# A graph network with attention and a tree of experts: fewer zero columns among the edge matmuls, zero matmuls behind the edges, and epsilon inside ScalarE's root

## The reference

```
xn = layernorm(x)
x1 = x + gnn(xn, 10000 random edges) + linear_attention(xn)
out = x1 + tree(layernorm(x1))

gnn, three layers:
    hn  = h @ Wn + bn
    m   = hn[src] + edge_attr @ We + be        # one row an edge
    agg = segment_sum(m, dst) / max(count, 1)
    h   = relu(layernorm(concat(hn, agg) @ Wc + bc) * gamma + beta)     # eps = 1e-5

tree: every row goes down 8 levels of a binary tree of 255 nodes; at each node it met it is
multiplied by that node's 256x256 matrix, weighted by gelu(|score|), and summed.
```

## Time and profile before

| | |
|---|---|
| median of 3 runs | 392.23 us (392.08 to 395.37) |
| the profiled execution, its own time | 393.82 us |
| its span, first to last instruction | 392.1 us |
| mean granted TensorE clock (1 is full) | 0.987 |
| PE busy | 357.6 us (91%) |
| DVE busy | 249.1 us (64%) |
| ACT busy | 149.5 us (38%) |
| POOL busy | 120.0 us (31%) |
| the chain that ended last: PE, DVE, DMA, ACT | 83%, 8%, 3%, 1% |

### The profile page before, as it was taken

One profiled execution on the slowest core, in us unless ns is written; L12 is line 12 of the kernel. 1 busy time (PEld: TensorE's weight loads), 2 busy tenths in 40 slices (PEclk: granted clock), 3 DMA queues, 4 the chain that ended last, 5 costly groups with the idle time before them and its releaser, 6 DMA issues.

```text
span 392.1 us, 9600 instructions
## 1 busy us (share of the span) xinstructions
PE 357.6 (91%) x2773; PEld 258.4 (66%) x2773; DVE 249.1 (64%) x678; ACT 149.5 (38%) x470; POOL 120.0 (31%) x241
## 2 busy tenths in 40 slices
PE   0599999999799999999977899999999999899966
PEld 0457778998688788876633466656656665566645
DVE  1637859991524335186796776669986666568732
ACT  1325536400301405004613356544556655444510
POOL 7200000700000000062650255456545554455510
PEclk9999999999899999998999899999999999999999
DMA  6931115730499900000071269999999999997001
GB/s 198 268 103 43 40 32 125 189 95 5 160 388 387 387 22 0 0 2 0 0 264 12 103 233 386 386 386 385 385 361 381 384 386 386 385 386 281 3 3 65
DMA packets 51785, 78.48 MB, mean 200 GB/s; under 512 B 3260, under 2 KB 19223, under 8 KB 51736
## 3 DMA queue, kind: packets, MB, share of 16 engines
q1 hardware_dynamic: 50506, 76.81, 56.3%
q10 hardware_dynamic: 1230, 1.05, 1.0%
HBM read 77.21 MB, written 0.64 MB: 199 GB/s over the span
## 4 chain that ended last, share of the span: by engine, by line
PE 83%; DVE 8%; issue 3%; DMA 3%; ACT 1%; SPq 1%; DVEq 1%; POOLq 0%; POOL 0%; ACTq 0%
PE ps L1280 80%; DMA reg<-in_L_gnn_Wc_dram 3%; PE ps L1283 2%; DVE reg L1270 1%; DVE reg L908 1%; DVE reg L1274 1%; DVE cols L1140 0%; SPq L401 0%; DVE reg L1134 0%; DVE reg_w L1220 0%; DVEq L361 0%; DVE colp L1146 0%; ACT reg L615 0%; DVE reg L1220 0%; ACT reg_w L624 0%
## 5 line engine op out<-in xcount | busy, mean ns | idle before, releaser
L1280 PE MATMUL ps<-reg 128*64 128x256 f32 (+6 forms) x1449 | 253.2, 315 | 7.0 <-DVE reg L1270 3.6
L1280 PEld LDWEIGHTS ps<-reg 128*64 128x64 f32 (+5 forms) x1449 | 176.1, 146 | 24.1 <-issue 7.8
L1280 PE MATMUL ps<-reg,reg_w 128*64 (+1 forms) x688 | 158.8, 388 | 4.9 <-DVE reg L1220 2.7
L1280 PEld LDWEIGHTS ps<-reg,reg_w 128*64 128x64 f32 (+1 forms) x688 | 94.2, 140 | 59.1 <-issue 14.9
L583 POOL TENSOR_TENSOR reg_w<-reg_w 128x128 f32 x150 | 72.9, 486 | 88.8 <-ACT reg_w L804 81.5
L1220 DVE SCALAR_TENSOR_TENSOR reg_w<-reg_w,nid,reg 128x128 f32 x167 | 65.4, 395 | 33.6 <-PE ps L1280 30.6
L803 ACT COPY reg_w<-ps 64x128 f32<-64x128 f32 x150 | 39.4, 262 | 68.4 <-PE ps L1280 68.3
L1220 DVE SCALAR_TENSOR_TENSOR reg<-reg_w,reg 128x128 f32 x150 | 50.9, 339 | 0.2 <-issue 0.2
L1280 PE MATMUL ps<-zeros_b 128*128 128x256 bf16 (+1 forms) x212 | 49.9, 302 | 0.0
L804 ACT COPY reg_w<-ps 64x128 f32<-64x128 f32 x150 | 39.0, 260 | 3.7
L908 DVE TENSOR_TENSOR reg<-iota,idxH 125x660 bf16<-125x660 f16 (+5 forms) x42 | 38.8, 993 | 0.0
(11 more groups left out here) (254 smaller groups left out, 297.8 us busy)
## 6 DMA issues: line engine op xcount, KB each, us to landing
reg<-in_L_ffn_w2s_dram SPq DMA_DIRECT2D x127, 512.0 KB, 11.5
reg<-in_edge_attr_dram SPq DMA_DIRECT2D x13, 336.0 KB
reg<-in_L_gnn_Wc_dram SPq DMA_DIRECT2D x3, 512.0 KB, 9.3
reg<-in_L_gnn_Wn_dram SPq DMA_DIRECT2D x3, 256.0 KB, 5.8
xin<-in_x_dram ACTq DMA_DIRECT2D x1, 512.0 KB
out_dram<-reg SPq DMA_DIRECT2D x4, 128.0 KB
reg<-in_edge_attr_dram SPq DMA_DIRECT2D x13, 39.0 KB
reg<-in_L_mix_w_qkv_dram ACTq DMA_DIRECT2D x1, 384.0 KB, 7.5
```

Source lines behind the costliest of these rows:

```text
L1280: return e.matmul(to, lhsT, rhs, start=start, stop=stop, skip_group_check=True)
```

## The change

Three edits.

1. `IDLE` goes from 256 to 160: the zero matmul between the two real ones of each of the 165 chunks has 96 columns fewer.
2. Behind the edges PE waits for `E_main` (ACT's copy of bank 7) and issues six matmuls of 512 zero columns into that bank, ahead of its wait for `E_ready`.
3. In the layers, ACT's root takes the variance straight from `mv`, and epsilon as its bias (a pointer to a column of `epsc`). DVE's addition of epsilon is gone, and its reciprocal now follows the root instead of preceding it. `l_r` is signalled by the mean-and-variance instruction, and `xhat` multiplies by `rv` in place of `rstd`. The LayerNorms before and after the layers are left as they were.

```diff
-IDLE = 256
+IDLE = 160
...
                 for i in range(NT):
                     e.wait_ge(l_r, l * NT + i + 1)
-                    e.activation(rstd[:, i:i + 1], rv[:, 1, i:i + 1], ACT.Sqrt).then_inc(l_sq, 1)
+                    e.activation(rstd[:, i:i + 1], mv[:, i, 1:2], ACT.Sqrt, bias=epsc[:, i:i + 1]).then_inc(l_sq, 1)
...
                 c(e.bn_stats(stats[:, i, :], ps[:, i, 0:D]))
                 c.wait()
-                c(e.bn_aggr(mv[:, i, :], stats[:, i, :]))
+                e.bn_aggr(mv[:, i, :], stats[:, i, :]).then_inc(l_r, 1)
+                e.wait_ge(l_sq, n)
+                c(e.reciprocal(rv[:, 1, i:i + 1], rstd[:, i:i + 1]))
                 c.wait()
-                c(e.tensor_scalar(rv[:, 0, i:i + 1], mv[:, i, 1:2], epsc[:, i:i + 1], None, ALU.add))
-                c.wait()
-                e.reciprocal(rv[:, 1, i:i + 1], rv[:, 0, i:i + 1]).then_inc(l_r, 1)
-                e.wait_ge(l_sq, n)
                 if l > 0:
                     e.wait_ge(l_t, n - NT)
-                e.tensor_scalar(xhat[:, i, :], ps[:, i, 0:D], mv[:, i, 0:1], rstd[:, i:i + 1], ALU.subtract,
+                e.tensor_scalar(xhat[:, i, :], ps[:, i, 0:D], mv[:, i, 0:1], rv[:, 1, i:i + 1], ALU.subtract,
                                 ALU.mult).then_inc(l_xh, 1)
...
+            e.wait_ge(E_main, 1)
+            for _ in range(6):
+                mm(ps[:, 7, :], zeros_b[:, 0:128], zeros_b[:, :], True, True)
             e.wait_ge(E_ready, 1)
             share_row(0).then_inc(p_c, 1)
```

## The result

The changed kernel takes **401.04 us** in the median of five executions (396.19 to 406.06), against 392.74 for five of the kernel before on the same chip. The ratio is 1.012, 95% interval [1.006, 1.018]: slower. The forecast was 389.7 (387.6 to 393.0), so it was wrong in its sign.

A forecast was written before the change was run, and what follows sets the result against it. PE's matmuls were taken to bound the kernel, with the edge loop paced by the sequencer. Columns 0, zeros -1.7 + 0.06, root -0.41 - 0.1 - 0.3 made -2.45, rounded to -2.5: from 392.23 to 389.7 us (387.6 to 393.0).

The forecast's parts named there:

- The loop is bound by the sequencer: Edge loop: the sequencer needs 0.20 us a chunk plus table loads and sets the pace, not the array's columns.
- The rule of the Trainium skill: Edge loop: a matmul of N columns takes N / 2.4 + 2.5 ns, giving 6.6 us less; rival at 383.1, chance 0.10.
- In the trace the loop runs at 1.00 with pauses up to 0.9 us: Edge loop: the remark closing the slower rival, in which the clock falls late in the loop; 393.7 us, chance 0.10.
- the rival priced at 393.7: Edge loop: the clock falls late inside it, costing 2.3 us against 0.8 gained in the layers; chance 0.10.
- the 0 at which the sum took the 160 columns: Edge loop: 96 fewer columns a chunk gain 0 us, within bounds of 0 and -6.6.
- The pause: Edge loop: with 160 columns the array idles about 1.1 us at each pause instead of 0.4.
- The fall: Late in the edge loop, in the slower rival: a clock fall of 3.4 us, costing 2.3 us.
- A fall early in the loop costs nothing much: Edge loop: at half clock a chunk takes 0.38 us against the sequencer's 0.20; the backlog is worked off later at 0.19.
- The six zeros: Behind the edges: clock kept at 1.00, -1.7 us, with share_row(0) 0.06 later; rival that it falls anyway, 391.5, chance 0.20.
- The root: Layers: pointer bias adds 0.09 us to the root, chain 0.16 shorter a tile; layers 0 and 1 gain 0.41 and 0.1.
- Both ends: Layer 2, root's gain: 0 if the clock falls within the twelve zeros, 0.62 us if not; 0.3 taken.
- The sum: Whole kernel: -1.7 + 0.06 - 0.41 - 0.1 - 0.3 = -2.45 us, rounded to -2.5, giving 389.7; chance 0.50.

The follow-up runs named there:

- the second execution: Second profiled execution of the changed kernel itself, all three edits: 397.68 us, with a clock fall of 13.7 us.
- last pause filled: Changed kernel (160 columns) plus four zero matmuls of 512 columns before the last load of the block table alone: 393.14 us, ratio 0.996 against the kernel before.
- the first execution: First profiled execution of the changed kernel itself, all three edits: 406.06 us, with a clock fall of 23.9 us.
- the run with the pause in the middle: Changed kernel with four zero matmuls before the last table load and the load before block 36 split in two: 401.20 us, ratio 1.015 against the kernel before.

## Why the prediction was wrong, step by step

**The loop is bound by the sequencer: right.** In the second execution PE's pauses end 5.87 and 5.74 us apart. Timeline of PE (idle before it, in brackets):

```profile
66.69 0.20 PE L1278 MATMUL ps<-reg 125*128 125x55 bf16 x1 [0.85 <-issue]
72.56 0.20 PE L1278 MATMUL ps<-reg 125*128 125x55 bf16 x1 [0.84 <-DVE reg L908]
78.30 0.20 PE L1278 MATMUL ps<-reg 125*128 125x55 bf16 x1 [0.74 <-issue]
```

(The bracket of the second row names DVE, whose matrices for that block were ready at 60.3 us; this pause is as long as the one before it.) The columns gave nothing at full clock: 40.30 us with 160 (last pause filled), 40.24 with 256, 44.9 with 352. The rule of the Trainium skill ("TensorE: Matmul & The Clock Gate", "Back-to-back issue gap") that the prediction set against it would have made the loop 6.6 us shorter; the loops of 40.30 and 40.24 us do not agree with that.

**"In the trace the loop runs at 1.00 with pauses up to 0.9 us": this step failed**, in the rival priced at 393.7 with a chance of 0.10, and with it the 0 at which the sum took the 160 columns. (The 0.9 us is the sequencer's lead; the pauses in the earlier trace rows are 0.12 to 0.68.) The columns alone made the median 2.8 us longer, 397.64 beside 394.85. Two sizes in the step were wrong.
- *The pause.* The prediction spoke of 1.1 us at each. The five in the middle are 0.74 to 0.85, but the last is 1.24 to 1.31. It stood in the earlier trace rows: the last pause was 0.68 already, behind the load of 1.33 us, and what comes off a piece (5.61 to 5.04, 0.57) is added to it: 1.25. The step looked at the typical pause and not at the longest.
- *The fall.* The prediction gave it 3.4 us, the length of the one in the earlier trace rows, and 2.3 us of cost. It lasted 13.7 and 23.9. Runs with 160 or 208 columns and a last pause of 1.1 us or more had falls of 13.7 to 23.9 us in six profiles of six; with 256 columns there was one of 3.4 us behind a pause of 1.57 and none behind one of 2.27. The one trace at hand had no fall within the loop to take a length from.

**"A fall early in the loop costs nothing much": wrong too.** At half clock a chunk takes 0.32 us, where the prediction had 0.38 (the matmuls of 160 columns start 0.32 apart in the first execution), the loop's pace is 5.90 / 24 = 0.246, so each chunk at half clock adds 0.07 us. Working that off needs the clock back before the loop ends. In the run with the pause in the middle it was not back: 8.7 us longer than 40.3, of which the second load of 1.47 us is a part that is not the clock's.

**The six zeros: right in size.** Alone they keep the clock at 1.00 behind the edges:

```profile
103.69 1.12 PE L1280 MATMUL ps<-reg,row 2*128 2x512 f32 x2
105.34 2.40 PE L1280 MATMUL ps<-reg 128*128 128x256 f32 x10 [0.53 <-ACT reg L699]
107.67 0.48 PE L1280 MATMUL ps<-reg,row 2*128 2x128 f32 x2
```

From `around(0, 0)` to `share_row(1)` it is 2.33 us, before 109.71 - 105.72 = 3.99: 1.66 less, where 1.7 was said. From the signal (101.44) to `share_row(0)` it is 2.25, 0.09 more, where 0.06 was said. No fall stood there in any profile with 256 or more columns and the zeros, save the one that a longer pause before them had brought; the kernels without them (before, root alone) have it in both profiles. The gain counts only while the clock is up when the zeros begin, and in the changed kernel it was down.

**The root: right in the trace, not shown in the time.** Groups of instructions of the changed kernel, to set beside the earlier trace rows:

```profile
L730 ACT ACTIVATE rstd<-mv,epsc 128x1 f32<-128x1 f32 x15 | 4.4, 295 | 49.7 <-DVE mv L1056 49.7
```

295 ns against 203: 0.092 for the pointer, and 0.09 was taken. That is also what the Trainium skill gives for one ("ScalarE: Activation LUTs", "What ACT_TABLE_LOAD costs"). From the signal at the loop's end to the twelve zeros of layer 2 the kernel before takes 74.21 us and the root alone 73.42 (174.81 - 101.39); with the zeros it is 72.62 without the root (174.06 - 101.44) and 71.87 with it (172.94 - 101.07). So the root gives 0.75 to 0.79 in layers 0 and 1, where 0.51 was said. In layer 2, between the first records of the two groups of zeros, it is 14.00 us without the root (188.06 - 174.06) and 13.39 with it (188.20 - 174.81) where the clock stays up: 0.61 against 0.62. Where it falls within the twelve zeros, 14.38 before and 14.51 with 256 columns: nothing. Both ends came true, each in its case. By the time the root alone gained nothing, and added to the zeros it went from 392.63 to 391.15 in the same batch, with intervals that overlap.

**The sum** of what was said for zeros and root was -2.5 us; the kernel with these two and 256 columns is 0.995 [0.992, 0.999] of before, that is 0.5 to 3.3 us faster. The forecast was in effect one for that kernel. The sign lay in a cut that gives no time and that I booked at 0 because nothing waits for the array. The columns had another use, which the earlier trace rows could have suggested: they kept PE busy.

**The falls in the tree** (3.4 us before, 10.2 in both profiles of the changed kernel) were not in the prediction. They are not the columns' doing: the kernel with 256 columns has 10.2 as well. With zeros in PE's gaps ahead of them they are gone, in three profiles of three.

**What stays open.** Why a fall lasts 3.4 us in one case and 27.3 in another: few columns and a long pause together went with the long ones, but the case of 256 columns rests on two profiles. Whether the moment of a pause counts beside its length: no run moved a pause of one length by small steps. Why executions of one program differ in their falls. And why the fall at 51 us, ahead of any difference between the programs, stands in seven of the ten profiles with 160 or 208 columns and in one of the ten with more. It cost 1.7 us where it stood, so a part of what the kernels with few columns lose may not be the last pause's.

## What to carry to other kernels

Before filler work is cut from an engine that waits for its sequencer anyway, ask what the filler keeps up; here 96 columns a chunk cost no time and held the clock. Look at the longest pause of PE and not at the usual one: what is taken off the work before a pause is added to it in full. And price a fall of the clock by the longest stretch that any run shows, not by the one in the trace at hand; a few zero matmuls in PE's gaps were worth more here (a ratio of 0.997 with those behind the edges alone, and from 0.995 to 0.988 with those in two gaps of the tree) than the instruction saved.

## What the runs showed of the hardware

- The load of table entries into PE's registers depends on where and how many: twelve entries from a multiple of twelve 0.85 us (1.03 for the first of the loop), eleven from entry 72 1.33, twelve from entry 71 2.87 and 2.88. Split in two, six entries took 0.83 and 0.84, then five from entry 78 1.24 and six from entry 42 1.47 us. The last has an even start and an even count, so oddness alone does not explain it; which property decides was not taken apart.
- A fall begun within the edge loop kept TensorE at the lower of its two levels (1.2 GHz) for up to 27.3 us while PE was busy for 27.07 of 27.20 us. Being busy did not bring the clock back in that time.
- The clock fell in or behind pauses of 1.14 to 2.78 us in this loop (eight profiles) and stayed up behind one of 2.27 (one profile, 256 columns).
